# Attention layer 1 with fp16 plane pairs, a quarter of its tiles turned by DMA

## What is computed

```python
def layer0(x, Wb, Wc, Wd, gamma):                       # x: (4, 256, 1024)
    B, C, D = (einsum('oc,bcn->bon', W, x) for W in (Wb, Wc, Wd))
    S = softmax(einsum('bcn,bcm->bnm', B, C), axis=-1)
    return gamma * einsum('bcm,bnm->bcn', D, S) + x

def layer1(x, ...):                                     # 4 heads of 64 channels
    hn = group_norm(x, 32 groups) * gamma + beta
    q, k, v = (conv1x1(hn, w, b) split into 4 heads)
    attn = softmax(einsum('bhdq,bhdk->bhqk', q, k) / 8, axis=-1)
    out = einsum('bhqk,bhdk->bhdq', attn, v)
    return x + conv1x1(out, wp, bp)
```

## Time and profile before

| | us |
|---|---|
| median of 3 runs | 682.38 |
| lowest and highest run | 681.85, 683.33 |
| the profiled execution, its own time | 682.95 |
| its span, first to last instruction | 681.0 |
| of the span: layer 0, then layer 1 from about | 0 to 245, 245 to 681 |

### The profile page before, as it was taken

The page is one execution under the profiler, slowest core; times in us unless marked ns, Lnnn a source line. Parts: engine busy times, 40 slices in busy tenths (PEclk is TensorE's granted clock), DMA queues, the critical chain, the costliest instruction groups (busy, mean ns, idle before and its releaser), DMA issues.

```text
span 681.0 us, 11125 instructions
## 1 busy us (share of the span) xinstructions
PE 668.9 (98%) x3668; PEld 568.5 (83%) x3668; DVE 560.4 (82%) x910; ACT 455.7 (67%) x790; POOL 231.2 (34%) x216
## 2 busy tenths in 40 slices
PE   8989999999999899999999999999999999999997
PEld 7878888888888778888888888888888888988886
DVE  4787768768678478998888899888899888889996
ACT  5563435435435167988787788777789778778884
POOL 0130211201125024565233465242546433334531
PEclk9999999999999999999999999999999999999999
DMA  7476856645645957001656010367110265301001
GB/s 227 85 134 188 170 99 138 155 100 128 165 97 123 213 141 203 1 1 48 146 119 185 17 47 1 93 155 193 54 54 8 58 157 126 92 16 47 1 32 62
DMA packets 96714, 69.50 MB, mean 102 GB/s; under 512 B 71072, under 2 KB 73376, under 8 KB 96672
## 3 DMA queue, kind: packets, MB, share of 16 engines
q1 hardware_dynamic: 96672, 68.97, 41.8%
HBM read 18.62 MB, written 8.39 MB: 40 GB/s over the span
## 4 chain that ended last, share of the span: by engine, by line
PE 86%; DVE 5%; issue 3%; ACT 2%; POOL 2%; DMA 1%; SPq 1%; POOLq 0%; DVEq 0%; ACTq 0%
PE acc L1410 36%; PE scores L1410 26%; PE trans L1444 16%; PE trans L1410 8%; DVE negmax L979 1%; ACT prob L739 1%; DMA x_raw<-in_x 1%; POOL planes L638 1%; DVE pt_lo L997 1%; ACT pt_hi L749 1%; DVE pt_lo L1168 1%; DMA turned<-planes 0%; POOL y_in L649 0%; SPq L466 0%; DVE qk L1132 0%
## 5 line engine op out<-in xcount | busy, mean ns | idle before, releaser
L626 POOL TENSOR_SCALAR prob<-prob,rsum 128x1024 f32<-128x1024 f32 x127 | 142.8, 1124 | 256.7 <-DVE rsum L984 256.7
L739 ACT ACTIVATE prob<-scores,negmax 128x1024 f32<-128x1024 f32 x160 | 178.9, 1118 | 74.4 <-DVE negmax L979 72.9
L979 DVE TENSOR_REDUCE negmax<-scores 128x1 f32<-128x1024 f32 x160 | 194.0, 1213 | 17.8 <-PE scores L1410 16.6
L749 ACT ACTIVATE pt_hi<-trans 128x512 fp32r<-128x512 f32 x256 | 139.6, 594 | 63.9 <-PE trans L1444 63.3
L997 DVE TENSOR_TENSOR pt_lo<-trans,pt_hi 128x512 fp32r<-128x512 f32 x256 | 163.5, 680 | 1.0 <-ACT pt_hi L749 0.6
L1410 PE MATMUL scores<-k_st,q_st 128*128 128x512 f32 x512 | 137.9, 391 | 0.7 <-issue 0.7
L1444 PEld LDWEIGHTS trans<-ident,prob 128*128 128x128 f32 x1024 | 117.7, 140 | 22.5 <-issue 4.2
L1444 PE MATMUL trans<-ident,prob 128*128 128x128 f32 x1024 | 134.6, 273 | 1.2 <-DVE pt_lo L997 1.1
L1410 PEld LDWEIGHTS scores<-k_st,q_st 128*128 128x128 f32 x512 | 95.7, 188 | 21.6 <-issue 1.2
L1410 PE MATMUL acc<-pt_hi,v_st 128*128 128x512 f32 (+1 forms) x264 | 106.8, 407 | 0.6 <-DVE pt_lo L997 0.6
L1410 PE MATMUL acc<-pt_lo,v_st 128*128 128x512 f32 (+1 forms) x264 | 101.0, 385 | 0.0
(11 more groups left out here) (163 smaller groups left out, 1028.0 us busy)
## 6 DMA issues: line engine op xcount, KB each, us to landing
k_st<-qk SPq DMA_DIRECT2D x64, 256.0 KB, 4.7
q_st<-qk SPq DMA_DIRECT2D x64, 128.0 KB, 2.4
x_raw<-in_x SPq DMA_DIRECT2D x8, 512.0 KB, 5.2
y_out<-in_x SPq DMA_DIRECT2D x16, 256.0 KB, 3.3
y_scratch<-y_out SPq DMA_DIRECT2D x16, 256.0 KB, 2.3
y_in<-y_scratch SPq DMA_DIRECT2D x4, 1024.0 KB, 7.5
y_res<-y_scratch SPq DMA_DIRECT2D x16, 256.0 KB, 3.7
out<-y_res SPq DMA_DIRECT2D x14, 256.0 KB, 2.1
```

Source lines behind the costliest of these rows:

```text
L626: nc.gpsimd.tensor_scalar(p, p, rsum[:, t % 2:t % 2 + 1], 1.0, ALU.mult, ALU.mult)\
L739: nc.scalar.activation(prob[:, t % 2, :], scores[:, t % 2, :], ACT.Exp, bias=negmax[:, t % 2:t % 2 + 1], scale=1.0, accum_out=rowsum[:, t ...
L749: nc.scalar.activation(pt_block(pt_hi, (t // 4) % 2, t, h), trans[:, h, :].rearrange("p (j n) -> p j n", n=P), ACT.Copy).then_inc(pt_high, 1)
L979: nc.vector.tensor_reduce(negmax[:, t % 2:t % 2 + 1], scores[:, t % 2, :], AX_X, ALU.max, negate=True).then_inc(max_ready, 1)
```

## The change

Layer 1's probabilities and values are held as pairs of fp16 planes (high and low) in place of pairs of fp32r parts: `pt16` takes the place of `pt_hi` and `pt_lo`, `v_st` becomes fp16, and the `av` matmuls read fp16 on both sides. To fit fp16's range, the probabilities are multiplied by 32768 in `normalise`, and the weights of the values are scaled by powers of two that are worked out on the chip from bounds (new: `value_factors` on POOL behind the fifth tile of image 0, a small group `vb` on PE in front of `av0`, `value_scales` on DVE between the turned tiles and `result0` of image 0, one ACT copy); `output_rows` and `output_add` multiply by the inverse. The high and low part of the value weights leave the lead-in.

The first tile of every four (s % 4 = 0; not in the last four of the last image) is no longer transposed by PE: ACT makes its high plane (`plane1_high`), POOL its low plane (`plane1_low`, behind `normalise` of the next tile), and SP issues one DMA transpose of both planes straight into `pt16` (`turn1`). These tiles have no transposes on PE, no `trans_high` on ACT and no `trans_low` on DVE. `prob` has four buffers in layer 1, so the exponential waits for the tile four before. SP's list is written out for every image.

```diff
+TURNED = (0,)
+LOW_ON_VECTOR = ()
@@ tiles
-        pt_hi = sb("pt_hi", [P, 2, NT, H], F32R)
-        pt_lo = sb("pt_lo", [P, 2, NT, H], F32R)
+        pt16 = sb("pt16", [P, 2, 2, NT, H], F16)          # shares the room of pt_hi, pt_lo
+        prob_more = sb("prob_more", [P, 2, N])
-        v_st = sb("v_st", [P, NT, HEADS, 2, HD], F32R)
+        v_st = sb("v_st", [P, NT, HEADS, 2, HD], F16)
@@ SP
+            def turn1(i, t):
+                sp.wait_ge(low_plane1[t % 4 in LOW_ON_VECTOR], lows_before(i, t) + 1)
+                if t % 4 == TURNED[0]:
+                    sp.wait_ge(acc_done, GROUP_CREDIT + slot_free(i, t) + 1)
+                sp.dma_start_transpose(
+                    pt16[:, (t // 4) % 2, :, :, (t % 4) * P:(t % 4 + 1) * P].rearrange("p a j n -> p (a j) n"),
+                    flat(planes[:, turn1_slot(t), :, :])).then_inc(turned1[turn1_slot(t)], 16)
@@ POOL
+            def plane1_low(i, t):
+                pool.wait_ge(high_plane1, turned_before(i, t) + 1)
+                nc.gpsimd.tensor_tensor(planes[:, turn1_slot(t), 1, :], prob1(t), planes[:, turn1_slot(t), 0, :],
+                                        ALU.subtract).then_inc(low_plane1[False], 1)
             for t in range(T0_IMAGE):
                 high_plane(0, t)
+                if t == 4:
+                    value_factors()
...
                         normalise(T1_BASE + T1_IMAGE * i, s + 1)
+                    if is_turned(i, s) and s % 4 not in LOW_ON_VECTOR:
+                        plane1_low(i, s)
@@ ACT
+            def plane1_high(i, t):
...
+                act.wait_ge(prob_ready, T1_BASE + T1_IMAGE * i + t + 1)
+                nc.scalar.activation(planes[:, d % 2, 0, :], prob1(t), ACT.Copy).then_inc(high_plane1, 1)
...
-                    trans_high(t1, s, before)
-                    if s + LAG < T1_IMAGE or not plan.last:
-                        exp(t1, s + LAG)
+                    if is_turned(i, s):
+                        plane1_high(i, s)
+                    else:
+                        trans_high(i, s)
+                    if s + LAG < T1_IMAGE:
+                        exp1(i, s + LAG)
+                    elif not plan.last:
+                        exp1(i + 1, s + LAG - T1_IMAGE)
@@ DVE
                 turned_low(0, t)
+            value_scales()
             for a in range(2):
                 result0(0, a)
...
-                    trans_low(t1, s)
+                    if not is_turned(i, s):
+                        trans_low(i, s)
@@ PE
+            pe.wait_ge(v_factors, 10 + KT)
+            group(plan0(0), "vb", [(v_spread[:, k, :], wv_size[:, k, :]) for k in range(KT)], slice(0, C))
             d_split(0)
             values0(0, "av0")
...
-                    pe.wait_ge(pt_split, SPLIT_CREDIT + halves_before(t1) + 8 * (j + 1))
+                    pe.wait_ge(pt_split, SPLIT_CREDIT + splits_before(i, 4 * (j + 1)))
+                    for t in TURNED:
+                        pe.wait_ge(turned1[turn1_slot(4 * j + t)], turn1_count(i, 4 * j + t))
-                group(plan, name, [(v_st[:, b, j % 4, :, :].rearrange("p v d -> p (v d)"), src[:, j % 2, b, :])
-                                   for b in range(NT) for src in (pt_hi, pt_lo)], part=part, parts=parts)
+                group(plan, name, [(v_st[:, b, j % 4, :, :].rearrange("p v d -> p (v d)"), pt16[:, j % 2, plane, b, :])
+                                   for b in range(NT) for plane in range(2)], part=part, parts=parts)
...
-                    transpose_tile(t1, s, plan.last)
+                    if not is_turned(i, s):
+                        transpose_tile(i, s)
```

More of the change, by code:

```diff
@@ L579, in image1 @@
-                load_residual(i, 0)
-                for name in plan.names:
-                    if name.startswith("next_qk"):
-                        restack(plan, name)
-                    elif name.startswith("out"):
-                        store(plan, name, i)
-                load_residual(i, 1)
-            image1(0)
-            with sp.Fori(1, IMAGES - 1) as i:
+                if not plan.first:
+                    load_residual(i - 1, 1)
+                for s in range(T1_IMAGE):
+                    if is_turned(i, s):
+                        turn1(i, s)
+                    if s == 3 and not plan.last:
+                        sp.wait_ge(h_split, 4 * i + 4)
+                        load_y(i + 1)
+                    if s == 15:
+                        load_residual(i, 0)
+                    for name in ends(STEPS1[s - 1]) if s > 0 else []:
+                        if not plan.has(name):
+                            continue
+                        if "qk" in name:
+                            if name == "qk7" and plan.first:
+                                sp.wait_ge(y_stored, FREE_CREDIT + IMAGES * 64)
+                            restack(plan, name)
+                        elif name.startswith("prev_out"):
+                            store(plan, name, i - 1)
+                        elif name.startswith("out"):
+                            store(plan, name, i)
@@ L589, in _ @@
+                if plan.has("next_qk6"):
+                    restack(plan, "next_qk6")
+            for i in range(IMAGES):
                 image1(i)
-            image1(IMAGES - 1)
+            load_residual(IMAGES - 1, 1)
             for side, name in enumerate(EPILOGUE_OUT):
@@ L743, in trans_high, with exp1 @@
-            def trans_high(t0, t, av_before):
-                if t % 4 == 0 and av_before is not None:
-                    wait_acc(av_before)
+                nc.scalar.activation(dst, scores[:, t % 2, :], ACT.Exp, bias=negmax[:, t % 2:t % 2 + 1], scale=1.0,
+                                     accum_out=rowsum[:, column:column + 1]).then_inc(exp_ready, 1)
+            def exp1(i, s):
+                if plan1(i).first and s < 2:
+                    act.wait_ge(low_plane, T1_BASE + s + 1)
+                elif plan1(i).first and s < 4:
+                    wait_acc(plan0(IMAGES - 1).number("av1"))
+                elif (s - 4) % 4 in TURNED:
+                    act.wait_ge(low_plane1[s % 4 in LOW_ON_VECTOR], lows_before(i, s - 4) + 1)
+                else:
+                    act.wait_ge(transposed, TRANS_CREDIT + 2 * passed_before(i, s - 4) + 2)
+                exp(T1_BASE + T1_IMAGE * i, s, prob1(s), s % 4)
@@ L747, in trans_high @@
+            def trans_high(i, t):
+                if all(n in TURNED for n in range(t % 4)):
+                    wait_acc(slot_free(i, t))
                 for h in range(2):
[L748 to L750 removed]
+                    act.wait_ge(transposed, TRANS_CREDIT + 2 * passed_before(i, t) + h + 1)
+                    nc.scalar.activation(pt16_block(0, t, h), trans[:, h, :].rearrange("p (j n) -> p j n", n=P),
```

250 lines of the change are left out of this document (171 added, 79 removed).

## The result

The changed kernel takes 688.76 us (median of 5, 687.74 to 690.57); the kernel before, on the same chip, 683.33 us (681.85 to 684.57). The ratio is 1.0084, with a 95% interval of 1.0059 to 1.0108: **slower by 0.8%**, where 670 us had been forecast. The profiled execution took 689.51 us, against 682.95 before.

What follows compares the result with a forecast made beforehand. PE was taken to bound the kernel, with DVE and ACT full beside it in light steps. From 682.95 us, layer 1 wins 18.7 and layer 0 loses 5.9: 670.2, so 670 for the median; forecast 664 to 675, range 655 to 687.

Steps and rivals of the forecast that it cites:

- `value_factors`, "5.3 us, from 38.7 to 44.0": Layer 0, POOL between `high_plane` of tiles 4 and 5: passes take 5.3 us, next plane 2.3 later, cost 2.3.
- `value_scales`, "4.6, less 1.0 of slack": Layer 0, DVE ahead of `result0` and `a_low`: 4.6 us, image 1's scores 1.0 later anyway; layer 0 loses 5.9 in all.
- `vb`, "runs in that gap: nothing": Layer 0, PE's added group, run while PE waits for `d_lo` before `av0`: costs nothing.
- SP, "both move by 1 to 2 us and are needed two steps later or more: nothing": Layer 1, SP's queue: `turn1` ahead of `restack` and the next image's load delays both by 1 to 2 us, costing nothing.
- PE's saving, "0.89 + 0.11 = 1.0": Layer 1, each half head (four steps): 0.89 us of dropped transposes plus 0.11 from faster fp16 `av` matmuls.
- The rival "no faster": Layer 1: fp16 matmuls are no faster, 3.4 us less won, 673 us; inside the forecast's range, no chance of its own.
- The ring through GpSimd, 11.1 us for four steps: Layer 1 light blocks: exponential of tile 1 to tile 5 through `plane1_low` takes 11.1 us against today's 11.04; nothing won.
- The block of steps 12 to 15: Layer 1, the block with `norm_chunk` and `pair_low` between two `normalise`: ring 11.8 us against today's 11.3, lost 0.5.
- Heavy blocks, "the full 1.0 is won": Layer 1 blocks with extra PE groups: ring 13.2 us, PE 13.9, so PE's full 1.0 us saving is won.
- the rival on that side: Layer 1: POOL's `plane1_low` is slow and the kernel slower, 684 to 705 us; turning point 3.2 us; chance 0.18.
- "Eaten in part": Layer 1: DMA transposes meet `restack` traffic and land late, 8 us lost over heavy blocks, 678 us (676 to 683); chance 0.15.
- the three signs: Forecast wrong if light blocks run under 10.5 us, `plane1_low` is over 3, or PE waits on the transposed planes.

Runs made afterwards that it cites:

- experiment 1: Changed kernel with `value_factors` run on GpSimd before its first probability plane instead of behind the fifth: 684.14 us, ratio 1.0011.
- experiment 2: On top of experiment 1, `value_scales` except its first pass moved behind image 1's `a_low`, ScalarE's copy likewise behind its `a_high`: 678.53 us, ratio 0.9930.
- experiment 4: Changed kernel with `av1` of layer 0's last image in bank 2 instead of bank 0: 686.20 us, ratio 1.0041.
- experiment 8: Changed kernel with SP issuing each layer 1 turn one step later, behind that step's restacks and stores, except the very first: 684.67 us, ratio 1.0025.
- experiment 5: Changed kernel with no tile turned by DMA; TensorE transposes every tile, fp16 planes and value scaling stay: 697.80 us, ratio 1.0215.
- experiment 9: Changed kernel with the three corrections together, those of experiment 2 (includes experiment 1), experiment 4 and experiment 8: 672.83 us, ratio 0.9828.
- experiment 10: Kernel of experiment 9 with GpSimd making only 512 of 1024 columns of each low plane, so part is not computed: 670.83 us, ratio 0.9796.
- experiment 11: Kernel of experiment 9 with the turned tile's high plane made by GpSimd instead of ScalarE's copy: 674.22 us, ratio 0.9867.
- experiment 12: Kernel of experiment 9 with image 1's load right behind the first turn, ahead of the restacks of `qk6` and `qk7`: 675.36 us, ratio 0.9892.

## Why the prediction was wrong, step by step

- **`value_factors`, "5.3 us, from 38.7 to 44.0".** It took 9.1 (from 37.67). The two one-input passes over 512 columns were priced by `norm_chunk`'s 0.89; here they took 2.35 and 1.94. Two of the passes over two columns took 1.05 and 0.77 in place of 0.20. The rest of the mechanism, the plane of tile 5 late and `d_lo` and `av0` behind it, was right: 5.2 us hang on it (experiment 1), not 2.3.
- **`value_scales`, "4.6, less 1.0 of slack".** It took 5.3 (62.03 to 67.33 in the changed kernel): the reciprocal of 256 columns is 1.75, not 0.42. Of the 10.8 us of layer 0, 4.7 go when it is moved (experiments 1 and 2).
- **`vb`, "runs in that gap: nothing".** True for its products. That one more group turns the rotation of the banks for everything behind it, up to the transition 190 us later, was not looked at: 2.7 of the 3.1 us (experiment 4).
- **SP, "both move by 1 to 2 us and are needed two steps later or more: nothing".** This is the step that failed in layer 1: 4.4 us between two traces, 4.1 by the medians (experiment 8). The queue was named, but the wait at its head was not followed: a `turn1` that waits holds the restacks behind it, and a heavy block is where they are wanted. At the start of image 0 the same queue is short of time in any order tried.
- **PE's saving, "0.89 + 0.11 = 1.0".** The 0.11 was right: fp16 products start 0.216 apart and win some 0.13 a half head on TensorE (experiment 5). What failed is the overlap. The transposes' 0.89 also hid a wait: without them the first product of an `av` quarter stands right behind the scores, and there it waits for what VectorE has still to finish, mostly an accumulator bank to be emptied. In the eight turned steps of image 2 in the kernel of experiment 9 it starts 0.24 to 0.90 behind the last score, 3.7 us in sum where eight times the shortest would be 1.9. The profile names a pass of VectorE as the end of the wait in five of them; of the seventh block it says (weight loads, 535.24 to 549.42 us):

```profile
PEld acc L1610 <- DVE qk L1295: 0.4, 1, 0.4
```

  In the three blocks of image 2 in which TensorE is full (the second, third and seventh) 0.74, 0.96 and 0.72 were won with SP's order mended, and this wait takes 0.18, 0.11 and 0.17 there. It is read from the trace; no run moved it. The rival "no faster" put 3.4 us on the fp16 products: the products were faster, but experiment 5 shows +2.6 in place of -3.4, by waits behind VectorE; the likely cause, not tested, is the scaled output rows, which the forecast had left at 0.71.
- **The ring through GpSimd, 11.1 us for four steps.** The light block took 10.84, and light blocks won nothing or half a microsecond, as forecast in kind. But the forecast's reason, GpSimd's pass alone, was not the whole (experiments 10 and 11). The block of steps 12 to 15 won 0.55 where 0.5 was to be lost.
- **Heavy blocks, "the full 1.0 is won".** With SP's order mended, the eight blocks of image 2 win 0.31, 0.74, 0.96, 0.55, 0.01, 0.39, 0.72 and 0.78, against 1, 1, 1, -0.5, 0, 1, 1 and 1: 4.5 in place of 5.5. In the changed kernel it was 0.30, 0.71, 0.95, 0.55, 0.00, 0.39, -0.24 and 0.64; the difference lies in the two blocks with q and k restacks. Of what is still missing, the wait above explains most in the second and the seventh. The first and the sixth lack 0.6 to 0.7 each; the same wait takes 0.2 and 0.4 of it, the rest was not followed further.
- **The rivals.** GpSimd's pass was not slow, so the kernel became slower by another way than the rival on that side. "Eaten in part" by the restacks was right in place, but through SP's order and not through the DMA engines: both planes landed after 4.3 us (median). A clock that falls was in no case of the forecast; it cost an estimated 2.6 us in the transition and at most 0.6 in layer 0.
- **The signs.** None of the three signs by which the forecast was to be known as wrong came: the light block took 10.84, `plane1_low` 2.15, and no wait of TensorE for a transposed plane is in the changed kernel's trace. They watched the new operations; the loss lay in what these hold up.

With the three corrections layer 1 wins 10.4 of the 18.7, and turning by itself 13.0 (the 2.6 of experiment 5 added). Of the 8.3 that are missing, 6.8 are image 0's (+1.3 in place of -5.5), 1.1 and 1.0 those of images 1 and 2; image 3 won 0.6 more than forecast. What image 0 lacks is 2.6 lost over tiles 0 to 12, where SP's queue is late with the restacks and the next input (experiment 12 shows that moving one delays the other), and a smaller gain behind them, whose cause was not followed.

## What to carry to other kernels

Where a change adds a wait to an in-order queue, list what stands behind it, and price that by when each of those is wanted, not by the few microseconds it moves. A small one-off preparation belongs where its engine is idle and behind what others wait for: moving two of them here was worth ten microseconds, more than half of what the change had been credited with in its main loop. And where buffers are dealt out by a rotation, one more customer changes who waits for whom far behind it: compare the assignment before and after. Work that is taken off an engine may have hidden a wait: ask what the instruction that moves up will find.

## What the hardware showed that was not expected

- **fp16 products next to fp32 ones.** fp16 products of 512 columns start 0.216 us apart, fp32 ones 0.2275. At the switch from fp16 to fp32, as from transposes to fp32 products, the first product behind it is recorded 0.03 us behind the one ahead of it and pays in its own time (0.42 and 0.31 to the next). A pace read from one group's start to the next group's is wrong there; the sum over both groups is not.
- **GpSimd's one-input passes** over 512 columns took 2.35 and 1.94 us in `value_factors` and 1.95 and 1.94 in experiment 1, where nothing waits behind them, against 0.89 in `norm_chunk`. They take a maximum or minimum and a product with numbers from the instruction; `norm_chunk` takes a product and a sum with numbers from a tile. Which of the two counts, no run parts. A two-input pass over the same tiles took its usual 1.26.
- **The price of a fall of TensorE's clock** to 0.50, its lower level of 1.2 GHz, was not the time at half pace, but what of it was still missing when the next engine was ready: 0.6 us or less in layer 0, an estimated 2.6 in the transition.
- **SP's queue as a resource.** Eight restack DMAs take 8 us of issuing, a turn of both planes 1.3 to 1.9. The Trainium skill ("Trainium Kernel Development and Optimization", Key Constraints) says that issuing from several engines only saves the sequencer's issue time; in this kernel that time, and its order, were worth some 4 us. Issuing the turns from another engine was not tried.
